# Parting the last down-projection of a feed-forward stage by tokens, and its sums and final transfer by channel

## The reference

```
def _mx_linear(x2d, w):
    return _mx_dequant(x2d) @ _mx_dequant(w).T
gate = _mx_linear(x2d, gate_w)
up = _mx_linear(x2d, up_w)
h = jax.nn.silu(gate) * up
out = _mx_linear(h, down_w)
...
x = x + _L1_ffn_ref(_L1_cond2_ref(x, ...), L1_ffn_gate_w, L1_ffn_up_w, L1_ffn_down_w)
```

## Time and profile before

| | |
|---|---|
| median of 3 runs | 3898.58 us |
| lowest, highest | 3896.74, 3898.66 us |
| profiled execution, its own time | 3897.72 us |
| its span in the trace | 3895.9 us |
| TensorE busy | 3377.4 us (87%) |
| VectorE busy | 2628.3 us (67%) |
| ScalarE busy | 1196.1 us (31%) |
| mean granted TensorE clock | 0.92 |

### The profile page before, as it was taken

How to read it: one execution, slowest core, us unless ns; L and a number is a source line. 1 busy time by engine, 2 the same in 40 slices (tenths; PEclk the granted TensorE clock), 3 DMA queues, 4 the chain that set the end, 5 groups by cost and what they waited for, 6 DMA issues and landing times.

```text
span 3895.9 us, 36828 instructions
## 1 busy us (share of the span) xinstructions
PE 3377.4 (87%) x12493; PEld 2062.0 (53%) x12493; DVE 2628.3 (67%) x3705; ACT 1196.1 (31%) x1953; POOL 510.5 (13%) x404
## 2 busy tenths in 40 slices
PE   1879879879878999999999588998889888988898
PEld 1554554554655777777777435543454345434643
DVE  7878878888875777888888255664566456646563
ACT  2333332332322545433433133122222222123310
POOL 1003003003003111111111202110202021201100
PEclk9989889889889999999999797999889988998799
DMA  4213212212104778778787510321013201320011
GB/s 146 67 40 65 65 32 64 63 32 56 52 29 150 263 245 273 244 258 278 244 278 241 226 39 1 117 105 55 33 76 114 86 33 76 110 90 33 16 49 43
DMA packets 276636, 436.67 MB, mean 112 GB/s; under 512 B 52320, under 2 KB 189536, under 8 KB 263904
## 3 DMA queue, kind: packets, MB, share of 16 engines
q1 hardware_dynamic: 256768, 379.85, 29.3%
q0 software_dynamic: 19680, 54.46, 4.4%
HBM read 364.59 MB, written 93.77 MB: 118 GB/s over the span
## 4 chain that ended last, share of the span: by engine, by line
PE 65%; DVE 21%; DVEq 5%; ACT 4%; issue 2%; DMA 2%; POOL 1%; SPq 0%; ACTq 0%; POOLq 0%
PE bank L1020 12%; PE bank L1049 7%; PE bank L1288 6%; PE bank L836 4%; PE bank L1301 4%; PE bank L1309 4%; PE bank L1217 3%; PE bank L1157 3%; PE bank L976 2%; PE bank L1195 2%; DVE sb_gla L1896 2%; PE bank L1026 2%; PE bank L816 2%; PE bank L813 2%; PE bank L1253 2%
## 5 line engine op out<-in xcount | busy, mean ns | idle before, releaser
L1020 PE MATMUL bank<-sb_xT,sb_work 128*128 128x256 f32 x2304 | 512.5, 382 | 1.6 <-issue 0.8
L1020 PEld LDWEIGHTS bank<-sb_xT,sb_work 128*128 128x128 f32 x2304 | 438.8, 192 | 75.1 <-issue 17.5
L836 PE MATMUL bank<-sb_gla,sb_work 128*128 128x256 f32 x896 | 265.9, 451 | 106.7 <-DVE sb_work L1898 94.2
L1049 PE MATMUL bank<-sb_work,sb_hT 128*128 128x512 f32 (+1 forms) x666 | 296.1, 592 | 0.0
L836 PEld LDWEIGHTS bank<-sb_gla,sb_work 128*128 128x128 f32 x896 | 193.5, 223 | 170.0 <-DVE sb_work L1898 113.0
L816 PE MATMUL bank<-sb_hT,sb_work 128*128 128x512 f32 x384 | 186.6, 635 | 86.4 <-DVE sb_hT L1837 86.4
L1301 PE MATMUL bank<-sb_parts,sb_gla 128*128 128x512 f32 x512 | 237.7, 608 | 4.5 <-ACT sb_gla L1634 4.5
L1288 PE MATMUL bank<-sb_work,sb_parts 128*128 128x512 f32 x512 | 233.9, 617 | 2.7 <-ACT sb_work L1647 2.7
L1309 PE MATMUL bank<-sb_parts,sb_gla 128*128 128x512 f32 x512 | 230.8, 593 | 6.3 <-DVE sb_work L2497 6.3
L1692 POOL DMA_INDIRECT sb_parts<-scratch_h,sb_small x111 | 122.0, 1099 | 820.5 <-DMA sb_small<-scratch_ids 805.9
L1157 PE MATMUL bank<-sb_parts,sb_hT 128*128 128x512 f32 x512 | 228.7, 606 | 0.0
(11 more groups left out here) (391 smaller groups left out, 5938.0 us busy)
## 6 DMA issues: line engine op xcount, KB each, us to landing
sb_work<-scratch_gu SPq DMA_DIRECT2D x63, 1408.0 KB, 7.2
sb_parts<-scratch_mx SPq DMA_DIRECT2D x16, 3072.0 KB, 11.6
sb_work<-moe_w SPq DMA_DIRECT2D x63, 512.0 KB, 6.3
scratch_y<-sb_work SPq DMA_DIRECT2D x48, 512.0 KB, 7.6
sb_parts<-scratch_fq SPq DMA_DIRECT2D x24, 1024.0 KB, 8.7
sb_work<-w_qkvg SPq DMA_DIRECT2D x64, 256.0 KB, 2.5
scratch_gu<-moe_w SPq DMA_DIRECT2D x32, 512.0 KB, 5.8
sb_parts<-fT SPq DMA_DIRECT2D x48, 256.0 KB, 5.3
```

The lines of the kernel that those rows point to most:

```text
L836: mm = pe.matmul(dst.rearrange("p (h n l) -> p h n l", h=HPC, l=size), kS[u % 2][:, k * P:(k + 1) * P], late[:, :, k, :, 1, :], start=True ...
L1020: mm = pe.matmul(dst, egu[j % 3][:, which * NC + k, m * P:(m + 1) * P], xt[j % 2][:, k, :], start=(k == 0), stop=(k == NC - 1))
L1049: mm = pe.matmul(bank(YB[s]), einter[j % 2][0:n, a:a + P], edn[j % 3][0:n, m * D:(m + 1) * D], start=(m == 0), stop=(m == EC - 1))
```

## The change

`f_downs` gets a range of tiles. In each batch the last block's down-projection is issued in two parts: tiles 0 to 2 (384 moving columns) ahead of the transposes of tile 15, and tile 3 (128 columns) after them. The second part counts up `f_down` after each bank, not once at the end. VectorE's four sums each wait for their own bank. The next batch's small projection waits for one sum before each of its three banks. The last output transfer is cut into four, one for each chunk of channels, each after its sum.

```
-        f_down = ev("f_down", FB)
+        f_down = ev("f_down", FB - 1 + NC)
...
                     if b and m == 3:
-                        sp.wait_ge(f_down.sem, f_down.at(b - 1, FB))
+                        sp.wait_ge(f_down.sem, f_down.at(b - 1, FB - 1 + NC))
...
-            sp.wait_ge(x4_ready.sem, x4_ready.at(NB - 1, NC))
-            sp.dma_start(out[NB - 1], r3(X2[(NB - 1) % 2][:, :], T)).then_inc(stored.sem, 16)
-            sp.wait_ge(stored.sem, 16 * NB)
+            for oc in range(NC):
+                sp.wait_ge(x4_ready.sem, x4_ready.at(NB - 1, oc + 1))
+                sp.dma_start(out[NB - 1][:, oc, :], ch(X2[(NB - 1) % 2], oc)).then_inc(stored.sem, 16)
+            sp.wait_ge(stored.sem, 16 * (NB - 1 + NC))
...
-                else:
-                    pe.wait_ge(x4_ready.sem, x4_ready.at(b - 1, NC))
                 for i, (a, n) in enumerate(((0, 64), (64, 64), (128, 128))):
+                    if b:
+                        pe.wait_ge(x4_ready.sem, x4_ready.at(b - 1, i + 1))
                     for k in range(NC):
                         mm = pe.matmul(bank(i, n), wm6[:, k, a:a + n], ch(hT, k), start=(k == 0), stop=(k == NC - 1))
                 mm.then_inc(s_proj.sem, 1)
+                if b:
+                    pe.wait_ge(x4_ready.sem, x4_ready.at(b - 1, NC))
                 pe.wait_ge(ld_sw.sem, ld_sw.at(b, 4))
...
-                def f_downs(ib):
-                    pe.wait_ge(f_hT.sem, f_hT.at(b, (ib + 1) * NT))
+                def f_downs(ib, a=0, e=NT):
+                    pe.wait_ge(f_hT.sem, f_hT.at(b, ib * NT + e))
+                    t = slice(a * P, e * P)
                     for oc in range(NC):
                         for i in range(4):
-                            mm = pe.matmul(bank(oc), fw[ib % 2][:, 2, i, oc * P:(oc + 1) * P], hqT[ib % 2][:, i, :],
-                                           start=(ib == 0 and i == 0), stop=(ib == FB - 1 and i == 3))
-                    mm.then_inc(f_down.sem, 1)
+                            mm = pe.matmul(bank(oc)[:, t], fw[ib % 2][:, 2, i, oc * P:(oc + 1) * P], hqT[ib % 2][:, i, t],
+                                           start=(ib == 0 and i == 0), stop=(ib == FB - 1 and i == 3 and e == NT))
+                        if e == NT and (ib == FB - 1 or oc == NC - 1):
+                            mm.then_inc(f_down.sem, 1)
...
+                f_downs(FB - 1, 0, NT - 1)
                 f_transposes(FB * NT - 1)
-                f_downs(FB - 1)
+                f_downs(FB - 1, NT - 1, NT)
...
-                dve.wait_ge(f_down.sem, f_down.at(b, FB))
                 for oc in range(NC):
+                    dve.wait_ge(f_down.sem, f_down.at(b, FB - 1 + oc + 1))
                     x = ch(X2[b % 2], oc)
                     tt(x, x, bank(oc), ALU.add).then_inc(x4_ready.sem, 1)
```

## The result

The changed kernel takes 3861.57 us in the median of four runs (3858.24 to 3864.73), against 3898.62 us before (four runs). The ratio is 0.9901, with a 95% interval of 0.9884 to 0.9919: 37.1 us less, where 42.7 us less was forecast (3855.9 us, range 3848 to 3867). It is faster by 1.0%, clear of the interval, and the time lies in the range; the forecast was 5.7 us too low. The profiled execution took 3864.73 us, its span is 3862.9 us.

What follows compares the result with a forecast made beforehand. Bound: at four batch ends TensorE's wait for tile 15, the sums and a 1 MB transfer stand in a row. Changes of batch 30.6 plus end 12.1 give 42.7 us less, 3855.9 us, range 3848 to 3867.

Steps and rivals of the forecast that it cites:

- Step 1: Last block's down-projection, tiles 0 to 2: 32 passes of 384 columns take 10.30 us and cover VectorE's quantisation.
- Step 2: Between the two parts: transposes and copy of tile 15 stay exposed, 1.28 us.
- Step 3: Tile 3's part: 32 passes of 128 columns, 3.57 us until the next instruction, 3.84 us to the last result.
- The changes of batch: Three batch ends into the next small projection: it starts 10.1, 10.4 and 10.1 us earlier, 30.6 us together.
- The end: Last batch: last result 8.4 us earlier, sums 1.9 us less, transfer 1.8 us less, 12.1 us together.
- The waiting costs twice: TensorE's wait for tile 15 at batch ends costs again through the low clock, 2.8 us the second time.
- The sum: Whole kernel: 30.6 + 12.1 = 42.7 us less, giving 3855.9 us, 1.1% less.
- The clock didn't fall between the parts: Rival: the clock falls in the gap, the 128-column part costs 6.35 us, time 3875; chance 0.08.
- nor in the first: Rival: the whole parted down-projection runs at the low clock, +11.8 us, 3910; chance 0.02.
- a 384-column pass costs less than one of 512: Rival: in the first part a 384-column pass costs as much as one of 512, 3869.6; chance 0.03.
- the changes of batch did give: Rival: the three changes of batch give nothing, only the end does, time 3886.5; chance 0.04.
- One sign of being wrong: The prediction is wrong if the time from the small projection to the next batch end has grown.

Runs made afterwards that it cites:

- parting by tokens: The kernel before with the down-projection parted, but sums waiting for all of it, one small-projection wait and one output transfer: 3869.15 us, ratio 0.9926.
- the first series: The changed kernel's first timing against the kernel before: 3861.57 us, ratio 0.9901.
- the second's: The changed kernel timed again with no edit, against the kernel before: 3856.43 us, ratio 0.9892.
- the third's: The changed kernel timed once more, on another kernel's chip and beside its runs, against the kernel before: 3858.14 us, ratio 0.9888.

## Why the prediction was right, and where it was off

- *Step 1, the 384-column part.* 10.42 us from its start to the transposes, forecast 10.30. A pass took 0.323 us from start to start, just as on the line between 128 and 512 columns; 0.10 us of the 0.12 is the first pass behind a wait (0.427 us). VectorE's quantisation lay inside the part.
- *Step 2, transposes and copy:* 1.29 us (2651.72 to 2653.01), forecast 1.28.
- *Step 3, the 128-column part:* 3.77 us to the next instruction, forecast 3.57. The passes went at 0.112 us as forecast; the 0.2 us are two edges that the term left out, 0.10 us in the first pass behind the wait and 0.09 us between the last pass and L1120. The 3.84 us of the earlier trace rows held the first of them, and the prediction took all of the 0.27 us above 3.57 for the tail. The whole way from the copy to L1120 was thus 15.48 us, not 15.15.
- *The changes of batch:* 9.8, 10.1 and 9.7 us, forecast 10.1, 10.4 and 10.1. The small projection waited for no sum. The fourth weight load wasn't late: L1160, which needs it, has no bracket behind L1120.

```profile
2667.32 7.03 PE L1160 MATMUL bank<-sb_parts,sb_hT 128*128 128x512 f32 x16
```

- *The end:* 11.9 us, forecast 12.1. Cutting the transfer gave 1.8 us of it. The Trainium skill (DMA: Bandwidth & Descriptors, Anatomy of one DMA) fitted its figures to transfers that GpSimd issues, and these are SyncE's. The size-free part that it gives is there in kind, since a quarter of the bytes took 2.0 us and not a quarter of 3.8; an estimate by its figures is 2.6 us for 256 KB and 4.4 us for 1 MB, and here the rows decide. The prediction was wrong in saying that by that rule the end would gain 0.6 us less: it set the rule's 2.6 us against the rows' 2.0 but left the 3.8 us as they were. With the rule on both sides the difference is 1.8 us, the same as by the rows.
- *The waiting costs twice:* of the 41.6 us, filling the wait alone gives 9.6, by the clock; moving useful work into it gives the other 20 of the 29.7 us that parting by tokens is worth; sums and transfer give 11.3 to 11.8.
- *The sum:* 41.6 us in the ends against 42.7 forecast. The 1.1 us are steps 1 and 3. The other 4.5 us of the miss are not in any step: the first series' difference was 37.1 us, the second's 42.6 and the third's 39.7 (3897.87 to 3858.14), around the same ends. By the means of the same runs they were 38.5, 40.9 and 40.7 us. I had allowed the clock's falls 5 us to either side, and the miss is of that size; that it was the clock is shown for one stage of the first profile and not for the whole.
- *The rivals.* The clock didn't fall between the parts, nor in the first; a 384-column pass costs less than one of 512; the changes of batch did give. None of the four came about. One sign of being wrong did show in the first profile: the stretches from a small projection to the next batch end took 1154.6 us together against 1152.1 before. In the second profile they took 1149.3, so the new order alone does not do it.

Open: why an execution meets the falls where it does. That the first stage's 6.7 us are the clock's is shown by its rows; what decides them isn't. Two and three profiles of a kernel are also too few to exclude that the earlier batch ends shift the stretches behind them by a microsecond or two.

## What to carry to other kernels

Before work is moved into a wait, read the clock behind the wait: an engine that idles there may pay again when it resumes, and the price is in the rows. When a consumer waits for the last of several tiles, look also at which tile its first part waits for: here two tiles instead of three started the work 0.85 us earlier and still covered VectorE's quantisation. And for a gain near the spread of the runs, measure the stretch that the edit touches in the trace: here each of the four repeated within 0.1 us where whole times moved by 20. Before a slower stretch elsewhere is laid to an edit, see whether it lies ahead of the first changed instruction.

## What the runs showed of the hardware

With nothing changed in the instructions, the first batch's 48 passes of L1160 took 20.81 us in one execution and 23.40 in another, and the 16 ahead of them 7.06 and 9.77, with the granted clock at 0.50 and 0.53 in two windows of the slower one while TensorE was busy in the whole of each. An idle of 1.44 us stood ahead of them in both executions. With 12 passes in a wait of 5.8 us the clock stayed at 1.00 in the down-projection behind it, which took 14.00 us; with the wait empty it was 0.50 at the start, and the same passes took 15.67. A first pass behind a wait took 0.10 us longer than the next ones, at 128 and at 384 columns. Four transfers of 256 KB, issued 0.9 us apart, landed 2.0 us after their issue in the median; one of 1 MB took 3.8 us.
